# A graph-network kernel: in layer 1's source-order softmax pass, the second head's products move from VectorE to GpSimd, and the long scan is cut in two by head

## The reference

```python
h = (x @ W_lin + b_lin).reshape(N, HEADS, EMB)              # HEADS = 2, EMB = 64
ee = (edge_attr @ W_edge + b_edge).reshape(-1, HEADS, EMB)
x_i = h[src]
x_j = h[dst] + ee
alpha = (x_i * att_i).sum(-1) + (x_j * att_j).sum(-1)
alpha = jnp.where(alpha >= 0, alpha, NEG_SLOPE * alpha)
amax = jax.ops.segment_max(alpha, src, num_segments=N)
e = jnp.exp(alpha - amax[src])
denom = jax.ops.segment_sum(e, src, num_segments=N)
alpha = e / (denom[src] + 1e-16)
messages = x_j * alpha[:, :, None]
out = jax.ops.segment_sum(messages, src, num_segments=N)
out = out.mean(axis=1) + bias
```

## Time and profile before

| | us |
|---|---|
| median of 3 runs | 12264.19 (12244.66 to 12286.42) |
| the profiled execution | 12198.77 |
| its span in the profile | 12196.6 |
| the source-order pass, first products to last scan | 5558.6 to 6398.0 |
| one chunk of it (two parts and the next scores) | 30.57 |

### The profile page before, as it was taken

How to read it: one execution, slowest core, us unless ns; L and a number is a source line. 1 busy time by engine, 2 the same in 40 slices (tenths; PEclk the granted TensorE clock), 3 DMA queues, 4 the chain that set the end, 5 groups by cost and what they waited for, 6 DMA issues and landing times. The chain is left out here.

```text
span 12196.6 us, 91756 instructions
## 1 busy us (share of the span) xinstructions
PE 3418.8 (28%) x20557; PEld 2882.3 (24%) x20557; DVE 6935.0 (57%) x9433; ACT 4568.1 (37%) x5711; POOL 6748.7 (55%) x6626
## 2 busy tenths in 40 slices
PE   1111566667100000000004366666665400000002
PEld 1111556566100000000003244545444300000001
DVE  6766565555322111127993377777776566666664
ACT  1111334334121111115770366666665134434432
POOL 7777544344577777770002556666654166666663
PEclk9999766666555555555555566566666655555555
DMA  3232312111232222224541333434343266666662
GB/s 98 75 77 77 74 57 61 48 49 60 31 109 104 102 103 102 99 96 168 207 192 31 82 110 110 117 110 117 110 117 91 94 201 198 206 204 200 205 200 85
DMA packets 722784, 1395.94 MB, mean 114 GB/s; under 512 B 409552, under 2 KB 439453, under 8 KB 715095
## 3 DMA queue, kind: packets, MB, share of 16 engines
q0 software_dynamic: 287072, 587.19, 18.1%
q1 hardware_dynamic: 406642, 636.11, 15.5%
q10 hardware_dynamic: 28996, 171.86, 4.0%
HBM read 827.48 MB, written 602.51 MB: 117 GB/s over the span
## 5 line engine op out<-in xcount | busy, mean ns | idle before, releaser
L794 POOL DMA_INDIRECT l_rows<-in_x,l_idx x1568 | 1740.4, 1110 | 1288.0 <-DVE r_hot_high L281 766.9
L1875 POOL DMA_INDIRECT l_rows<-h,l_idx x1568 | 1539.0, 981 | 1033.1 <-DMA l_idx<-sorted_src 560.0
L2386 POOL DMA_INDIRECT l_rows<-table,l_idx x1568 | 1482.8, 946 | 1028.9 <-issue 506.2
L1261 POOL DMA_INDIRECT rows<-l_rows,l_idx x1568 | 1609.0, 1026 | 569.4 <-issue 541.8
L1904 PE MATMUL l_made<-l_kv_w,l_rows_t 97*128 97x256 f32 x3136 | 1297.2, 580 | 992.2 <-ACT l_kv L1934 548.7
L1904 PEld LDWEIGHTS l_made<-l_kv_w,l_rows_t 97*128 97x128 f32 x3136 | 874.4, 296 | 1275.0 <-issue 1109.2
L2462 ACT ACTIVATE l_lifted<-l_rows,l_up 128x256 f32<-128x256 f32 x1568 | 653.5, 462 | 806.1 <-DVE l_half_low L2414 527.8
L1652 PE MATMUL l_wide<-l_diag,l_ones 128*128 128x384 f32 x4 | 3.3, 928 | 3293.0 <-DVEq L1682 3293.0
L1250 DVE TENSOR_TENSOR l_rows<-l_run,l_weights_ps 128x56 f32<-128x56 f32 x56 | 12.0, 215 | 1472.7 <-POOLq L88 1105.8
L1221 ACT COPY l_rows<-l_run 128x1792 f32<-128x1792 f32 x56 | 190.7, 3405 | 1710.2 <-POOLq L88 1275.4
L1652 PEld LDWEIGHTS l_wide<-l_diag,l_ones 128*128 128x128 f32 x4 | 1.0, 313 | 3293.9 <-DVEq L1682 3293.9
(11 more groups left out here) (375 smaller groups left out, 13289.9 us busy)
## 6 DMA issues: line engine op xcount, KB each, us to landing
sums<-l1s_out ACTq DMA_DIRECT2D x56, 1988.0 KB, 6.8
sums<-l_out SPq DMA_DIRECT2D x112, 924.0 KB
spread<-zeros SPq DMA_DIRECT2D x28, 3612.0 KB
l_spread<-spread SPq DMA_DIRECT2D x112, 903.0 KB
l1s_rows<-rows SPq DMA_DIRECT2D x56, 1008.0 KB, 4.8
spread<-zeros SPq DMA_DIRECT2D x56, 938.0 KB
l_spread<-spread SPq DMA_DIRECT2D x56, 938.0 KB
sums<-l_out ACTq DMA_DIRECT2D x56, 896.0 KB
```

The source lines that it names most:

```text
L794: pool.indirect_dma_start(rows[:, b, t], None, a["x"], bass.IndirectOffsetOnAxis(ap=idx[:, b, t:t + 1], axis=0)) \
L1261: pool.indirect_dma_start(g["rows1_d"], bass.IndirectOffsetOnAxis(ap=idx[:, b, t:t + 1], axis=0), rows[:, b, t], None).then_inc(sent[b], 16)
L1875: pool.indirect_dma_start(rows[:, c.r, t, 0:C], None, g["h2_d"], bass.IndirectOffsetOnAxis(ap=idx[:, c.r, t:t + 1], axis=0)).then_inc(got[ ...
L2386: pool.indirect_dma_start(rows[:, b, t], None, g["table3_d"], bass.IndirectOffsetOnAxis(ap=idx[:, b, t:t + 1], axis=0)) \
```

## The change

Per part, VectorE makes only the first head's product, into a PSUM tile `data` of half the size. GpSimd makes the second head's product into a new SBUF tile `data_last`, which has one buffer for each part. The scan of 2 x 70 x 29 values becomes two of 70 x 29, head 0 from PSUM and head 1 from `data_last`, with a wait for GpSimd's semaphore `weighed` between them. The copy of the running sums into column 0 becomes two. SyncE waits for `weighed` too before it loads a part's rows again. GpSimd waits for the chunk's exponentials (`exp_ready`) and for the scan that last read its buffer (`scanned`). Apart from that, `Normalise` objects of layers 0 and 1 are merged into one, which uses four semaphores fewer and counts on in the second layer; it changes no instruction but the values waited for.

```diff
-        data = s.ps("l1s_data", [P, H, F, T + 1])
+        data = s.ps("l1s_data", [P, F, T + 1])
+        data_last = s.sb("l1s_data_last", [P, PARTS, F, T + 1])
...
                     for n in range(PARTS):
                         wait(sp, rows_used[c.b][n], c.h + 1)
+                        wait(sp, weighed[n], c.at + 1)
                         sp.dma_start(rows[:, c.b, n * T:(n + 1) * T].rearrange("p t w -> p (t w)"),
...
                         at = slice(n * T, (n + 1) * T)
-                        for head in range(H):
-                            last = v.tensor_tensor(data[:, head, :, 1:].rearrange("p f t -> p t f"), rows[:, b, at, 0:F],
-                                                   exp[:, b, 1, head, at].unsqueeze(2).to_broadcast([P, T, F]), ALU.mult)
-                        last.then_inc(rows_used[b][n], 1)
-                        v.tensor_copy(data[:, :, :, 0:1], run[:, 1 - n, :, :, T:T + 1])
+                        v.tensor_tensor(data[:, :, 1:].rearrange("p f t -> p t f"), rows[:, b, at, 0:F],
+                                        exp[:, b, 1, 0, at].unsqueeze(2).to_broadcast([P, T, F]), ALU.mult).then_inc(rows_used[b][n], 1)
+                        v.tensor_copy(data[:, :, 0:1], run[:, 1 - n, 0, :, T:T + 1])
+                        v.tensor_copy(data_last[:, n, :, 0:1], run[:, 1 - n, 1, :, T:T + 1])
                         wait(v, scale_ready[n], c.at + 1)
                         wait(v, copied[n], c.at + 1)
                         v.drain()
-                        v.tensor_tensor_scan(run[:, n].rearrange("p h f t -> p (h f t)"), scale[:, n].rearrange("p h f t -> p (h f t)"),
-                                             data[:].rearrange("p h f t -> p (h f t)"), 0.0, ALU.mult, ALU.add).then_inc(scanned[n], 1)
+                        v.tensor_tensor_scan(flat(run[:, n, 0]), flat(scale[:, n, 0]), flat(data[:]), 0.0, ALU.mult, ALU.add)
+                        wait(v, weighed[n], c.at + 3)
+                        v.tensor_tensor_scan(flat(run[:, n, 1]), flat(scale[:, n, 1]), flat(data_last[:, n]), 0.0, ALU.mult, ALU.add).then_inc(scanned[n], 1)
                         v.drain()
...
+            @block.gpsimd
+            def _(pool):
+                pool.wait_ge(set_up, 1)
+                for c in chunks(pool, NB):
+                    wait(pool, exp_ready[c.b], c.h + 2)
+                    for n in range(PARTS):
+                        at = slice(n * T, (n + 1) * T)
+                        wait(pool, scanned[n], c.at + 1)
+                        pool.tensor_tensor(data_last[:, n, :, 1:].rearrange("p f t -> p t f"), rows[:, c.b, at, 0:F],
+                                           exp[:, c.b, 1, 1, at].unsqueeze(2).to_broadcast([P, T, F]), ALU.mult).then_inc(weighed[n], 1)
```

More of the change, by code:

```diff
@@ L158, in build @@
         node_w, edge_w, node_const = keep_tile("l1_node_w", [P, 2, H, F1 + 1]), keep_tile("l1_edge_w", [P, H, D5]), keep_tile("l1_const", [P, H])
+        norm = Normalise(sem, "l01")
         ordering(nc, a, sem, dict(locals()))
@@ L941, in layer0 @@
             work, stat = s.sb("l0_work", [P, NT, C]), s.sb("l0_stat", [P, 3, NT])
-            norm = Normalise(sem, "l0")
+            norm = g["norm"]
             with nc.Block() as block:
@@ L1301, in layer1 @@
             zeroed = sem("l1n_zeroed")
-            norm, pairs = Normalise(sem, "l1"), Pipeline(sem, "l1n", 2, PAIRS)
+            norm, pairs = g["norm"], Pipeline(sem, "l1n", 2, PAIRS)
             with nc.Block() as block:
@@ L1314, in _ @@
                     v.drain()
-                    norm.vector(v, acc, acc, x, work, stat, 1)
+                    norm.vector(v, acc, acc, x, work, stat, 2)
                 @block.scalar
@@ L1320, in _ @@
                     pairs.scalar(act, [lambda n, tiles: nc.scalar.copy(turned_s[0:F1, n % 2, 0:len(tiles) * H * P], turned[0:F1, n % 2, 0:len(tiles) * H * P])])
-                    norm.scalar(nc, act, acc, work, stat, 1)
+                    norm.scalar(nc, act, acc, work, stat, 2)
                 @block.tensor
@@ L1384, in source_order_sums @@
         rows_used = [two(f"rows_used{b}_") for b in range(2)]
-        scale_ready, scanned, copied, stored = (two(n) for n in ("scale_ready", "scanned", "copied", "stored"))
+        scale_ready, scanned, copied, stored, weighed = (two(n) for n in ("scale_ready", "scanned", "copied", "stored", "weighed"))
         set_up = sem("l1s_set_up")
@@ L1404, in _ @@
                         v.sem_inc(rows_used[b][n], 1)
+                    v.sem_inc(weighed[b], 2)
                     v.sem_inc(exp_ready[b], 1)
```

## The result

The changed kernel takes 12341.57 us (median of 8 runs, 12314.81 to 12386.44), the kernel before 12283.16 us in 8 runs beside it (12244.66 to 12288.12). The ratio is 1.0058 (that of the means of the runs; the two medians are 58 us apart), 95% interval 1.0042 to 1.0073: it is slower by about 71 us, and the interval goes from 52 to 90 us. The forecast was +141 us.

The account below looks back on a forecast made before the run. VectorE was taken to bound the pass. Per chunk, -3.6 us saved plus 4.04 and 4.6 for two exposed GpSimd products gives +5.04, over 28 chunks +141 us: 12264 + 141 = 12405 us, range 12250 to 12490.

Parts of the forecast that it names:

- the likeliest case: Both of a chunk's GpSimd products hold up VectorE at the scores: 12335 to 12480 us, chance 0.66.
- VectorE's saving: In the pass, one product less, with split scan and copies counted: -1.8 us a part, -3.6 a chunk, -101 us in all.
- The bound: VectorE, busy 290.15 of 300 us, bounds the changed pass; ScalarE's chain of 23.7 us a chunk stays below.
- Where GpSimd's products fall: Both of a chunk's products ask for their turn when part 1's second scan ends, where the scores begin.
- Exclusion in both directions: VectorE instructions with two SBUF inputs and GpSimd's work shut each other out; those with a PSUM input run freely.
- The second product gets in as well: Queued behind the first, it enters among the scores at a drain and holds up VectorE for 4.6 us a chunk.
- How long one product takes: GpSimd's product of 1960 values: 4.6 us, the middle of 3.7 (two streams) and 5.5 (three).
- What a pair costs: At the start of the scores, VectorE pays 4.04 us for the first product and 4.6 for the second, each chunk.
- the prediction's own formula: A chunk changes by 2W - 0.56 - 3.6 us, W being one GpSimd product's time; it turns at 2.08 us.
- GpSimd would not hold VectorE: VectorE goes on beside a running GpSimd product, the scores keep 3.7 us: 12163 us, chance 0.18.
- only one product would be exposed: The second product runs beside the first head's scan from PSUM: +0.7 us a chunk, +20 us, 12284, chance 0.14.
- the loads keep their cover: The side load lands at 5914.1, the scores want it at 5918.53: 4.4 us to spare.

Follow-up runs that it names:

- the undisturbed kernels: Changed kernel with GpSimd's product left out, or run one part ahead beside the first head's scan: 26.03 us a chunk each, ratios 0.9876 and 0.9912.
- the later session: Three kernels against the one before (10830.08 us): split with both products in PSUM 1.0009, second in SBUF 1.0081, GpSimd one part ahead 0.9899 (10720.24 us).
- the memset: Changed kernel with GpSimd's product replaced by a memset of the same 70 x 28 values: 27.26 us a chunk, one execution of 12167.38 us.

## Why the prediction was right, and where it was off

The direction and the mechanism were right, the size was twice what was measured: +141 us forecast, +71 measured. The time of 12341.57 us lies in the stated range, at the low end of the likeliest case's own (12335 to 12480). By the chunks (28 x 2.38 = 67 us) the sum is 74 us too high: 47 for the length of GpSimd's product, 13 for VectorE's saving and 14 for how much of a pair is paid.

- **The bound.** VectorE bounds the pass, and nothing else took over: right. In the changed kernel ScalarE waits more than before (259.8 us against 190.2), and what the undisturbed kernels save on VectorE is found again in the time (114 us by the chunk, 110 between the medians of the later session).
- **VectorE's saving** was put at 3.6 us a chunk and is 4.07 (chunk of 30.10 less 26.03). The split was costed at +0.15 us, the copies at +0.1 and the wait at +0.05 a part. Between the parts' scans the timeline has 13.41 us before and 11.35 after, which is 2.06 less, nearly all of the product's 2.11: the two scans overlap by 0.08 us, and the extra copy and wait are hidden. Two small terms of the sum, the 0.05 us for the wait and 0.1 us for the handing over, were estimates that no run shows; measured were 0.0 us of idle time ahead of the second scan, and 0.19 us from the end of a scan to the start of the memset that waits for it.
- **Where GpSimd's products fall**: right, both at the end of the second scan of part 1, where the scores begin.
- **Exclusion in both directions**: right. GpSimd holding VectorE is shown by the pair that VectorE waits out, by the cost following GpSimd's work (6.45 us for the whole, 2.93 for half), and by its being gone when the same work runs beside a scan with PSUM data (26.03 us a chunk, as with the product left out). VectorE holding GpSimd is shown by the first product of each pair, 6.01 us beside the scan of two SBUF tiles against 3.75. That GpSimd holds VectorE was an assumption before the change: in layer 0, where POOL issues gathers all the while, the 56 products took 3.19 to 3.33 us and the 56 scans 4.02 to 4.03 us. One thing went beyond the rows: they show the conflict for instructions with two SBUF inputs alone, and the sum applied it to the start of the scores as well. The two instructions held there, L1419 and L1420, read a single tile. That they are held too was first seen in the changed kernel. And the reading of the earlier trace rows did not hold for a GpSimd instruction that only writes: the scan of two SBUF tiles did not keep the memset of 1.73 us out.
- **The second product gets in as well**: right. It did not need a drain of the scores: it went in between the first two instructions, or while the first was still held.
- **How long one product takes** is the term that was most mis-sized: 4.6 us, the middle of the estimates for two and for three streams, where it is 3.76 (3.74 and 3.75 in the timelines above). The estimate for two reads at the IOTA's rate, 3.7 us, came out, and the step from it to the middle was the error. Why it comes out is not shown: that the two reads follow each other was assumed, and the memset, which reads nothing, takes 1.73 us for as many values.
- **What a pair costs.** With 3.76 us and the saving of 4.07 the prediction's own formula gives 2 x 3.76 - 0.56 - 4.07 = 2.89 us a chunk against 2.38 measured, because a pair costs 6.45 us and not 6.96. The 0.66 us of idle time that the formula takes off stands ahead of the scores of every fourth chunk only; the mean of 26 chunks is 0.31, before and after. Against that, the pair ends 7.1 us behind the scan and not 7.5, and 0.38 us of work on L1419 and L1420 falls into the same time: L1420 ends 7.2 us behind the scan instead of 0.7, which is 6.5. That 7.15 - 0.66 of one chunk gives 6.5 too is chance.
- **Rivals.** That GpSimd would not hold VectorE is refuted. That only one product would be exposed did not occur. It was also said that the loads keep their cover: in the changed kernel they do, while the kernel that runs GpSimd beside its own part's scan lost it, and pays 1.5 us a chunk.

## What to carry to other kernels

When work goes from VectorE to GpSimd, the question is not whether GpSimd has time but beside which VectorE instruction it will run, and what both read and write. Beside GpSimd's product, VectorE's product of two SBUF tiles was held here even with its output in PSUM (5.56 us instead of 2.20), and so were copies and a `tensor_scalar` from SBUF to SBUF (3.79 and 3.42 us in the timeline above, instead of 0.23 and 0.24). The scan that reads one tile from SBUF and one from PSUM (4.38 us), and the `tensor_scalar` from SBUF into PSUM (0.32 us), were not. Other forms were not tried. In this kernel the change cost 71 us with the product beside the scores, and gained about 110 us when waits on existing semaphores moved it beside the scan with PSUM data (with the exponentials taken earlier on ScalarE). Here the sign of the clash was an instruction of 0.24 us that showed 4.98 us on average, without a wait.

## What the runs showed of the hardware that was not expected

- VectorE's product of 1960 fp32 values with a written step of 29 values takes 2.20 us into PSUM and 3.66 us into SBUF (1.12 and 1.87 ns a value). GpSimd writes the same pattern into SBUF in 3.76 us, about VectorE's time.
- The clash depended on both sides: the GpSimd memset of 1.73 us ran beside a scan of two SBUF tiles at no cost (4.36 us), but held a copy from SBUF to SBUF (1.66 us instead of 0.23). A copy of two values per partition waited for a whole product (3.63 us on average, with `hold_keep` in PSUM).
- The pass is equal to 0.1% in two sessions (33.07 and 33.07 us a chunk, 26.03 and 26.02), while the kernel before takes 12187 us in one and 10830 us in the other. What differs lies in other stages, and was not followed up.
